# A selective scan with routed experts: three phases over time in place of three phases over channels

## What is computed

```python
xz = x @ in_proj_w.T                     # x: layer norm of h, 2 * 192 channels out
x_branch, z = jnp.split(xz, 2, axis=-1)
u = silu(causal depthwise convolution of x_branch, 4 taps)
dt = softplus(u @ dt_w.T + dt_b)
Bv = u @ B_w.T; Cv = u @ C_w.T           # 16 states
dA = exp(dt[..., None] * A)
dBu = dt[..., None] * Bv[:, :, None, :] * u[..., None]
h = dA_t * h + dBu_t                     # over 384 tokens, per channel and state
y = einsum('bdn,bn->bd', h, C_t) + D_param * u
r = (y * silu(z)) @ out_w.T + residual   # then a layer norm with ln_g, ln_b
```

## Time and profile before

| what | value |
|---|---|
| times of three runs | 541.25, 545.41, 520.53 us; median 541.25 |
| the profiled execution | 521.7 us, span 519.9 us |
| granted TensorE clock, mean | 0.924 |
| PE, PEld busy | 438.6, 309.7 us |
| DVE, ACT, POOL busy | 294.1, 206.9, 215.0 us |
| chain that ended last | PE 53%, issue 21%, DVE 12%, POOL 5%, ACT 4%, DMA 3% |
| preparation, scan, output work, rest | 137.3, 136.8, 48.5, 197.3 us of the span |

### The profile page before, as it was taken

The page is one execution under the profiler, slowest core; times in us unless marked ns, Lnnn a source line. Parts: engine busy times, 40 slices in busy tenths (PEclk is TensorE's granted clock), DMA queues, the critical chain, the costliest instruction groups (busy, mean ns, idle before and its releaser), DMA issues.

```text
span 519.9 us, 7212 instructions
## 1 busy us (share of the span) xinstructions
PE 438.6 (84%) x2381; PEld 309.7 (60%) x2381; DVE 294.1 (57%) x497; ACT 206.9 (40%) x422; POOL 215.0 (41%) x169
## 2 busy tenths in 40 slices
PE   5787979999798867778778998699999999999920
PEld 4345636456543323334334687588999999999910
DVE  4400365374799999999992873814434344443232
ACT  1312183375465646654650132103444444444400
POOL 6777303000166656664661000423444444444232
PEclk9977998999989999998999997758999999999975
DMA  8110005800000000000004021001111111112053
GB/s 220 26 6 5 5 1 208 339 0 1 0 1 0 0 0 0 0 2 0 0 0 153 30 81 42 0 16 44 54 48 53 53 47 49 46 52 53 24 179 109
DMA packets 14817, 25.32 MB, mean 49 GB/s; under 512 B 4989, under 2 KB 11886, under 8 KB 13774
## 3 DMA queue, kind: packets, MB, share of 16 engines
q1 hardware_dynamic: 10446, 17.37, 9.7%
q0 software_dynamic: 4352, 7.71, 5.7%
HBM read 19.26 MB, written 5.80 MB: 48 GB/s over the span
## 4 chain that ended last, share of the span: by engine, by line
PE 53%; issue 21%; DVE 12%; POOL 5%; ACT 4%; DMA 3%; DVEq 1%; SPq 0%; POOLq 0%; ACTq 0%
PE ps L858 12%; PE ps L841 8%; DVE ps L1287 7%; PE ps L673 5%; PE ps L847 5%; PE ps L647 3%; PE ps L646 3%; DVE w_all L1296 3%; PE ps L817 2%; DVE state L1296 2%; POOL w_all L507 2%; PE ps L831 1%; PE ps L615 1%; PE ps L616 1%; POOL h_tok L550 1%
## 5 line engine op out<-in xcount | busy, mean ns | idle before, releaser
L507 POOL TENSOR_TENSOR hc<-state,x_cm 128x768 f32<-128x768 f32 x24 | 43.6, 1815 | 74.3 <-DVE state L1296 74.3
L1048 ACT ACTIVATE decay<-dt_cm,a_neg 128x766 f32<-128x766 f32 x48 | 44.8, 936 | 57.5 <-DVE state L1296 30.6
L543 POOL DMA_INDIRECT y_dram<-u_cm,tok_out x31 | 35.3, 1139 | 75.1 <-ACT u_cm L1135 73.0
L673 PE MATMUL ps<-cst 128*128 128x256 f32 x208 | 55.2, 428 | 6.8 <-DMA cst<-in_cst 5.5
L673 PEld LDWEIGHTS ps<-cst 128*128 128x128 f32 x208 | 44.4, 218 | 15.8 <-DMA cst<-in_cst 5.5
L507 POOL TENSOR_TENSOR w_all<-w_all,x_cm 128x768 f32<-128x768 f32 x24 | 43.6, 1817 | 22.7 <-DVE w_all L1296 22.7
L484 POOL DMA_INDIRECT w_all<-in_pix,gidx x42 | 43.2, 1030 | 14.7 <-issue 12.5
L1120 ACT ACTIVATE u_cm<-ps,x_cm 128x128 f32<-128x128 f32 x96 | 26.6, 377 | 55.2 <-PE ps L847 55.2
L1287 DVE TENSOR_TENSOR ps<-dtu_cm,ps 128x768 f32<-128x768 f32 x48 | 45.3, 944 | 4.0 <-PE ps L708 3.9
L719 PE MATMUL ps<-c_parts,pick 128*128 128x384 bf16 x96 | 24.9, 342 | 23.3 <-ACT x_cm L1056 23.3
L1296 DVE TENSOR_TENSOR_SCAN state<-decay,ps 128x768 f32<-128x768 f32 x24 | 42.1, 1754 | 2.7
(11 more groups left out here) (215 smaller groups left out, 750.8 us busy)
## 6 DMA issues: line engine op xcount, KB each, us to landing
w_all<-in_w_all SPq DMA_DIRECT2D x8, 1156.0 KB, 8.6
w_all<-y_dram SPq DMA_DIRECT2D x3, 768.0 KB, 6.5
x_dram<-dt_cm SPq DMA_DIRECT2D x3, 384.0 KB, 2.6
out<-h_tok SPq DMA_DIRECT2D x3, 384.0 KB, 2.6
w_all<-in_pix,gidx POOLq DMA_INDIRECT x42, 2.4
w_all<-in_i SPq DMA_DIRECT2D x2, 256.0 KB
dt_cm<-x_dram,tok_in POOLq DMA_INDIRECT x31, 2.8
y_dram<-u_cm,tok_out POOLq DMA_INDIRECT x31, 2.5
```

The lines of the kernel that those rows point to most:

```text
L507: nc.gpsimd.tensor_tensor(hcs[p], states[p], c_sb[p], ALU.mult).then_inc(hc_rdy, 1)
L543: pool.indirect_dma_start(y_dram, bass.IndirectOffsetOnAxis(ap=tok_out[:, i:i + 1].bitcast(U32), axis=0), y_out[:, i % 2, :], None).then_i ...
L673: nc.tensor.matmul(ps[:, bank, 0:256], ident, cst[:, 0:256], start=True, stop=True)
L1048: nc.scalar.activation(decay[:, p, :, 1:L], unit(dt3, US[n], 1, L - 1), ACT.Exp, scale=a_neg[:, g, bass.ds(s, 1)]).then_inc(decay_rdy, 1)
```

## The change

The scan runs in phases over time. A phase is one chunk of 128 tokens, all six blocks at once; the three phases have 16 steps each, 48 in all, written out with no hardware loop. Each block of a step has 130 columns (`SEG`), two more than its tokens: in the first the decay is 0, which separates the blocks, and the second brings in the state that the phase before had left (`carry`, saved by GpSimd, put into PSUM by ScalarE). The scan instruction is 780 columns wide.

- Phase 0 starts when chunks 2 (text) and 0 are prepared; the z projection, convolution, dt, B and C projections, split and softplus of the last chunk stand between its steps.
- Output projection, residual, layer norms, router rows, transposes, logits and the two largest of chunk n - 1 stand between the steps of phase n; only those of the last chunk come behind the scan.
- C rows no longer go through TensorE and ScalarE: the projected rows are stored in DRAM (`c_dram`) and each step's row is read back by three DMAs to all partitions, with a ring of three buffers (`RING`).
- D * u is a matmul with a diagonal (skip_term) into the same PSUM sums.
- Projections to dt, B and C take two batch items per matmul; the coarse levels go through the fusing weights before the interpolation, which is part of the token matmul; abs and relu of dt are both on ScalarE.
- Four of the eight experts are loaded in quarters between the C rows, three after the last sum, one after the last logits.
- `keep_warm` stays in three places only: at the start, before the slots, before the first tile.

The diff, cut to its core:

```diff
-LATE = 2
+LATE = 4
+SEG = P + 2
+WIDE = 6 * SEG
+RING = 3
+PIECES = 4
...
-        WARM = {"input weights": 10, "interpolated levels": 8, "fine tokens": 3, "last convolution": 10,
-                "last steps": 24, "router's rows": 32, "later rows": 3, "last rows": 2, "slots": 8, "first tile": 4}
+        WARM = {"input weights": 10, "slots": 8, "first tile": 4}
+        STEPS = NJ * S
...
@@ sync @@
+            def broadcast_c(at):
+                r = at % RING
+                if at >= RING:
+                    sp.wait_ge(hc_rdy, at - RING + 1)
+                sp.dma_start(c_sb[r][:, 0:4 * P], c_dram[at:at + 1, :].to_broadcast([P, 4 * P])).then_inc(c_ready[r], 16)
+                for half in range(2):
+                    sp.dma_start(c_sb[r][64 * half:64 * half + 64, 4 * P:6 * P],
+                                 c_dram[at:at + 1, 2 * P * half:2 * P * half + 2 * P].to_broadcast([64, 2 * P]))\
+                        .then_inc(c_ready[r], 16)
...
+            for at in range(RING, STEPS):
+                if at == S - 3:
+                    store_c(2)
+                if at == S:
+                    sp.wait_ge(c_stored, 16 * 8)
+                broadcast_c(at)
+                if at > S and at % S == 13:
+                    send_rows(at // S - 1)
+                if at % 2 and piece < PIECES * (E - LATE):
+                    load_expert(piece // PIECES, piece % PIECES, PIECES)
+                    piece += 1
...
@@ gpsimd @@
+            for at in range(STEPS):
+                pool.wait_ge(scanned, at + 1)
+                if at < STEPS - S:
+                    nc.gpsimd.tensor_copy(carry[:, at % S, :].rearrange("p (q o) -> p q o", o=1),
+                                          segments(states[at % 2])[:, :, SEG - 1:SEG]).then_inc(carry_saved, 1)
+                pool.wait_ge(c_ready[at % RING], 48 * (at // RING + 1))
+                if at >= 2:
+                    pool.wait_ge(summed, at - 1)
+                nc.gpsimd.tensor_tensor(segments(hcs[at % 2]), inner(states[at % 2]), segments(c_sb[at % RING]),
+                                        ALU.mult).then_inc(hc_rdy, 1)
...
+            def spread_b(at):
+                n, s, p = at // S, at % S, at % 2
+                if at >= 2:
+                    pe.wait_ge(scanned, at - 1)
+                else:
+                    pe.wait_ge(lead_set, 1)
+                if s == 0:
+                    pe.wait_ge(split_step, 5 * min(n + 2, 3))
+                o, b = inner(wide(p)), chunk(b_parts, n)
+                nc.tensor.matmul(o[:, 0:2, :], pick[:, 0, s, :], b, start=True, stop=True)
+                nc.tensor.matmul(o[:, 2:3, :], pick[:, 1, s, :], b[:, 0:1, :], start=True, stop=True)
+                nc.tensor.matmul(o[:, 3:4, :], pick[:, 1, s, :], b[:, 1:2, :], start=True, stop=True)
+                nc.tensor.matmul(o[:, 4:6, :], pick[:, 2, s, :], b, start=True, stop=True).then_inc(b_wide, 1)
...
@@ tensor: the scan @@
+            for at in range(STEPS):
+                n, s = at // S, at % S
+                spread_b(at)
+                if s == 2:
+                    skip_term(n)
+                if n == 0:
+                    if s == 0:
+                        pe.wait_ge(x_out, 3)
+                        project_low(1, 4)
+                    elif s == 1:
+                        project_high(1, 4).then_inc(z_ps, 1)
+                    elif s == 4:
+                        pe.wait_ge(z_ready, 3)
+                        dt_low(2)
+                    elif s == 7:
+                        pe.wait_ge(abs_rdy, 5)
+                        pe.wait_ge(linear_rdy, 5)
+                        dt_high(2)
+                    elif s == 8:
+                        b_and_c(2)
+                else:
+                    if s == 3:
+                        residual_rows(n - 1)
+                    elif s in (4, 5):
+                        out_projection(n - 1, 2 * s - 8)
+                        out_projection(n - 1, 2 * s - 7)
+                    elif s == 11:
+                        router_transposes(n - 1)
+                    elif s == 13:
+                        router_logits(n - 1)
+                if at >= 2:
+                    sum_states(at - 2)
...
@@ scalar @@
+            def decay_of(at):
+                n, s = at // S, at % S
+                if s == 0:
+                    act.wait_ge(dt_rdy, min(n + 2, 3))
+                if at >= RING:
+                    act.wait_ge(scanned, at - RING + 1)
+                o = inner(decay[:, at % RING, :])
+                nc.scalar.activation(o[:, 0:NB, :], chunk(dt3, n)[:, 0:NB, :], ACT.Exp, scale=a_neg[:, 0, s:s + 1])
+                nc.scalar.activation(o[:, NB:6, :], chunk(dt3, n)[:, NB:6, :], ACT.Exp, scale=a_neg[:, 1, s:s + 1])\
+                    .then_inc(decay_rdy, 1)
+
+            def bring_carry(at):
+                act.wait_ge(carry_saved, at - S + 1)
+                act.wait_ge(b_wide, at + 1)
+                nc.scalar.activation(segments(wide(at % 2))[:, :, 1:2],
+                                     carry[:, at % S, :].rearrange("p (q o) -> p q o", o=1), ACT.Copy).then_inc(carry_set, 1)
...
+            for at in range(STEPS):
+                n, s = at // S, at % S
+                if S <= at + 1 < STEPS:
+                    bring_carry(at + 1)
+                if at + 2 < STEPS:
+                    decay_of(at + 2)
+                if n == 0:
+                    if s == 2:
+                        gate_of(2, 4)
+                        convolved(2)
+                    elif s == 6:
+                        dt_halves(2, 0)
+                    elif s == 8:
+                        dt_halves(2, 1)
+                    elif s == 9:
+                        b_and_c_rows(2)
+                        exponential(2)
...
+                else:
+                    if s == 7:
+                        deviation(1 + 2 * n)
+                    elif s == 9:
+                        deviation(2 + 2 * n)
+                    elif s == 12:
+                        router_input(n - 1)
+                    elif s == 15:
+                        logits(n - 1)
...
@@ vector: the scan; state_step(at) is the drive multiply, then the scan instruction @@
+            for at in range(STEPS):
+                n, s = at // S, at % S
+                state_step(at)
+                if n == 0:
+                    if s == 1:
+                        convolution(2)
+                    elif s == 10:
+                        split(2)
+                    elif s == 12:
+                        softplus(2)
+                else:
+                    if s == 1:
+                        chunk_output(n - 1)
+                        if n == 1:
+                            dve.wait_ge(hb_rdy, NJ)
+                    elif s == 6:
+                        residual(n - 1)
+                    elif s == 8:
+                        new_h(n - 1)
+                    elif s == 10:
+                        router_rows(n - 1)
+                    elif s == 15:
+                        largest(n - 1)
```

965 lines of the change are left out of this document (451 added, 514 removed).

## The result

The changed kernel took 555.54 us (median of four, 552.97 to 558.1) beside 531.04 us for the kernel before (520.53 to 545.41); the ratio is 1.067 (1.058 to 1.075). The changed kernel is slower by 5.8 to 7.5%, outside my range of 493 to 541. The profiled execution took 552.97 us with a span of 551.2 us, against 521.7 and 519.9.

What follows compares the result with a forecast made beforehand. VectorE was taken to bound the scan while idling in the stages on either side. Start 105, length 186 and tail 27 sum to 318 against 322.6 us, so the profiled 521.7 us becomes 517, range 493 to 541.

Steps and rivals of the forecast that it cites:

- Start of the scan: Preparation up to the first scan step: starts at 105 us (97 to 113), 32 earlier, with 8 us for low clock.
- the 97 for a full clock: Preparation: the first scan step would come at 97 us if all matmuls ran at the full clock.
- The price of a call: Preparation, b, c and dt projections: a wide call of 250 to 262 columns costs about 0.57 us.
- Length, own work: VectorE in the scan: 48 steps of 2.68 us, 128.6 us, plus inserted work, together 161 us without waits.
- Length, VectorE beside GpSimd's multiply: Scan: VectorE's inserted SBUF work waits for the port at seven places, 0.85 us each, 6 us (0 to 13).
- Length, TensorE's queue: Scan: VectorE waits for what inserted pieces take over TensorE's reserve per step, 20 us (8 to 28).
- Steps 0 and 1 are covered by the convolution: Scan, phase 0: TensorE's inserted work at these steps adds no wait, within the 3 us for that phase.
- C by DMA, GpSimd's copies: Scan: C rows take 5.5 us with 6.2 us of cover, GpSimd's small copies are hidden; 0 us each.
- Tail: After the scan, output work of the last chunk alone: 27 us (24 to 30) against 48.5.
- The one with VectorE carrying all: Rival, scan: TensorE's pieces are absorbed and the clock stays high; 492 us, chance 0.30.
- the late C rows: Rival, scan: GpSimd's multiply waits for C rows that take over 6.2 us; 536 us at 8 us each, chance 0.12.
- The case of a low clock in the scan too: Rival: low clock in preparation, 16 us at most, and a third of the scan at half clock; 535 us, chance 0.16.

Runs made afterwards that it cites:

- e6_narrow_warm: Changed kernel plus 49 warm-up matmuls at five places in the preparation, each through 64 columns of the array instead of 128; 565.18 us, a single execution.
- e11_regroup: Changed kernel with its projection matmuls reordered only, the four of 128 rows first, then the four of 64; 554.17 us, ratio 0.996 to the kernel before.
- e1_before_cold: Kernel before without the warm-up matmul groups that the change removes; 558.44 us, ratio 1.008 to the kernel before.

## Why the prediction was wrong

- **Start of the scan, the step that failed.** "Four bursts of 2 to 4 us at half rate cost 8 us. At least 0 and at most 16." Measured: 23 over the forecast 105, 31 over the 97 for a full clock. I took the clock to fall to half after waits and to come back with the next busy stretch, from the earlier trace rows: 0.51 from 76 to 82 us, and 1.00 from 84 to 98 us with narrow work. There such work held a clock that was up, for 14 us; I read from it that it would raise one that is down. It didn't in this kernel: 17.5 us back to back at 0.50. That a busy stretch ends the low clock after 2 to 4 us was my estimate, and the changed kernel shows no such burst: in place of four the whole stage of 98 us ran at 0.50, 80.5 us of it busy. With warm-ups and the order unchanged (e6_narrow_warm, clock 0.87 from 64 us to the scan) the start came at 140.5 us, 107.4 less the 33.1, which is near the forecast; that is an estimate, as some warm-ups ran within the standstill. The price of a call held: 0.57 to 0.63 us at a clock of 1.00 (e6_narrow_warm). I had no term for calls side by side, so that the same start can also be had by order (e11_regroup) is not in the prediction at all.
- **What the deletion costs.** I had put the clock down to the deleted warm-ups. Half right: with 49 of them the start moves by 11 to 21 us; but the kernel before does without them at 0.8%. In that kernel without them (e1_before_cold) the clock rose within its own token matmuls, and its projections of 125 and of 512 columns ran at 1.00 (from 85.11 and 138.15 us). The change replaced all of these, the projections by calls of 256 that alternate in rows. Which replacement took the rise away is argued from runs of such shapes, and no run puts the old matmuls into the changed kernel.
- **Length, own work:** 128.6 + 32.7 us forecast; 48 x 2.67 = 128.2 and 32.3 measured. Right.
- **Length, VectorE beside GpSimd's multiply:** 6 us forecast (0 to 13), 9.9 measured as longer instructions, against the durations without GpSimd: mis-sized within its bounds. The run with half the multiply took 5.1 us of it away and 0.7 off the scan. That the two share a port was my reading and is in no trace; what is shown is the longer time beside the multiply. The low bound, GpSimd waiting instead, is seen in the first profile: its copy L564, begun at 178.23 us, 0.14 us after such an instruction of VectorE, took 0.85 us in place of 0.19.
- **Length, TensorE's queue:** 20 us forecast (8 to 28), 28.8 measured, just past the bound. The right mechanism and mostly the right places: four records of output projection stalled 0.93 where I had 1.4, logits 4.0 where I had 3.4. The transposes, 1.0 forecast, took 3.4: I had costed them at the full clock, and behind their own wait it was half (1.05 us per group, and 2.72 for the sum behind them). "Steps 0 and 1 are covered by the convolution" was wrong: step 1 of phase 0 waited 2.63 us behind the z projection at half clock.
- **C by DMA, GpSimd's copies:** 0 forecast, 0 measured (1.8 us waited once; the run without the rows within 0.1 us). The copy takes 0.217 us, beside VectorE.
- **Tail:** 27 forecast, 26.0 measured. Right, also that its TensorE work ran at a lower clock (0.74).
- **The rivals.** The one with VectorE carrying all is out (34.5 us idle), and so are the late C rows. The case of a low clock in the scan too, 0.16 of the chances, was put at 535 us. It had the right cause and half the size: 18 us over the forecast where 36 were measured, because I took 16 us as its most in the preparation. Its third of the scan at half clock was an estimate, near what ran: means of 0.78, 0.84 and 0.82 in the three parts are 0.50 for 44, 32 and 36% of the time and 1.00 for the rest.

## What to carry to other kernels

Read the granted clock and the distance between the starts of equal matmuls, not the busy share alone: a TensorE that the trace shows without gaps stood at the lower clock for 17.5 us here. That work held a clock (1.00 for 14 us in the earlier trace rows) did not mean that it raised one (0.50 for 17.5 us here). When channels split into 128 and 64, issue the 128-row parts together and then the 64-row parts so that neighbours lie in different halves of the array: that alone was worth 5.5 to 6% here. Work put between the steps of a pipeline that VectorE bounds cost here what TensorE's queue had to take at that step (28.8 us of waits; with 0.8 us more of work waits of 0.93 us became 1.81), so look for the engine with the least slack, and then for the step.
